# One fused Mamba-2 and FFN kernel: the same steps in a new order on all four engines

## The chip, the cores and the metric

The kernel runs on one core of a Trainium2 chip. The metric is the device time of one execution in microseconds (us). Before the change three runs took 968.83, 967.83 and 967.86 us; the median is 967.86 us.

## The reference, cut to what matters

The input is 4 sequences of 1024 rows with 256 numbers each. Two sublayers follow one another, each as `x + layernorm(f(layernorm(x)))`.

```python
# f of the first sublayer: a Mamba-2 block, chunks of the scan, 8 heads of 64, state 128
zxbcdt = u @ in_proj_kernel                     # 256 -> 1288: z, xBC, dt
xBC = silu(causal_conv1d(xBC, w, b))            # 4 taps
dt = softplus(dt + dt_bias); dA = dt * -exp(A_log)
Y = Y_diag(C, B, exp(segsum(dA)), x*dt) + Y_off(C, state, exp(cumsum(dA))) + x*D
y = Y * silu(z); y = y * rsqrt(mean(y*y) + EPS) * norm_weight
return y @ out_proj_kernel
# f of the second sublayer: gated FFN, 2048 hidden, weights packed in 4 bits with scales
gelu = 0.5 * gate * (1 + tanh(0.797885 * (gate + 0.044715 * gate**3)))
return (gelu * up) @ Wd.T
```

## The kernel before

**Blocks.** The 4096 rows are cut into blocks of 512, shifted by half a block, so there are 9 of them (`NBLK`); the first and the last have one half only. A block's attention part is done in two halves of 256 rows, with two chunks of 128 in each. The FFN of a block runs over 16 slices of the hidden size (`NT`). In the text "attention" stands for the Mamba sublayer.

**Steps.** Everything is written as steps with a name and a number, one function for each step and engine. An order, written out by hand as a string, says which steps an engine takes one after the other. `name:k<` belongs to the block before, `name:k` to this one, `name:k>` to the next and `>>` to the one after. `drive` runs the orders `FIRST`, then `ORDER` for i = 2 to 8, then `LAST`. `there` leaves out the steps of halves that don't exist. Each engine (TensorE "pe", ScalarE "act", VectorE "dve", GpSimd "pool") runs its own order; they meet only in semaphores. The DMA queue of SyncE has its own fixed list.

**Steps of the attention half j.** `stats1`, `xn`, `xt`, `xn_split` normalise and transpose the input. `ip:0` to `ip:2` (half 0) and `ip:3` to `ip:5` (half 1) are the input projection, `taps` and `conv` the convolution, `silu` its activation. `z` and `gate` are the gate's projection; `z:3` and `z:4` also give dt, which `dt_bias` and `softplus` finish. `cs`, `decays`, `ct`, `sums`, `exps`, `decay_sums` and `decay_matrix` make the decays; a DMA spreads the sums over the partitions. `gb`, `gb_copy`, `decayed_products`, `xtr`, `xdt`, `yo`, `yoff`, `yd`, `ydiag`, `st` and `state` are the scan; `yt`, `yt_split`, `square`, `out`, `stats2`, `ln2` the output projection, norm and residual; `x1n`, `x1t`, `x1_split` normalise and transpose for the FFN.

**Steps of the FFN slice n.** TensorE's `gu:n` makes gate and up. ScalarE's `gelu:n` reads the gate, VectorE's `inter:n` multiplies by up, ScalarE's `split:n` and GpSimd's `split:n` make the high and low parts, TensorE's `dn:n` multiplies with the down weights. `fin` and `ln4` close the block. Matmuls run in three passes over high and low parts. In the first stage `dq`, `scale` and `dl` unpack the 12 pieces of the FFN weights; `wi_split`, `wi_z`, `wo_split` and `wo_lo` split the other weights, `rates` prepares A.

**Banks.** PSUM has three banks for the attention (`mb`), three for gate and up (`fb`), two for the FFN's output (`db`). The n-th use of a kind in TensorE's `ORDER` takes bank n % 3 and waits for the reader of the use three before:

```python
m_bank = {use[:2]: mb[n % 3] for n, use in enumerate(m_uses)}
f_bank = {use[:2]: fb[n % 3] for n, use in enumerate(f_uses)}
```

So `up:n` waits for `gelu:n-1`, and gate n for `inter:n-2`. A few waits more that the text speaks of:

```python
def gelu(f, par, n):
    act.wait_ge(s["gate"], count("gate", f, n))
    wait_before(act, "lo", f, n - 2)          # GpSimd's split of two slices before
def ip(i, par, q):                            # TensorE
    if isinstance(i, int) and i == 0 and q == 3:
        pe.wait_ge(wi_ready, 2)               # VectorE's wi_split
```

Of the kernel before, what the change touches and what calls it, by code (L numbers as in the profile page):

```python
# [78 lines left out]
        decay_matrix:0 decay_matrix:1 decay_matrix:2 split:3< split:4< gb_copy:0 decay_matrix:3 gelu:5< split:5<  # L79
        yt_split:0 square:0 gelu:6< gelu:7< yt_split:1 split:6< xn_split:1 split:7< taps:3 square:1 gelu:8<  # L80
        gate:3 gate:4 dt_bias:1 gelu:9< split:8< taps:4 taps:5 gelu:10< split:9< gate:5 gelu:11< silu:3 silu:4
        silu:5 decay_matrix:4 decay_matrix:5 split:10< gb_copy:1 exps:1 decay_matrix:6 gelu:12< split:11<
        xn_split:0> decay_matrix:7 square:2 gelu:13< yt_split:2 split:12< gelu:14< split:13< gelu:15< split:14<
        square:3 yt_split:3 split:15< dt_bias:0> gate:0> x1_split:0 gate:1> x1_split:1 taps:0> taps:1> taps:2>""",
    "dve": """
        inter:0< decays:0 inter:1< conv:1 inter:2< conv:2 sums:0 xdt:0 decay_sums:0 inter:3< decay_sums:1
        inter:4< gb_copy:0 decay_sums:2 decay_sums:3 decayed_products:0 stats1:1 yoff:0 ydiag:0 inter:5<
        decayed_products:1 state:0 yt_split:0 xdt:1 stats2:0 xn:1 yoff:1 ln2:0 ydiag:1 inter:6< inter:7< state:1
        yt_split:1 xn_split:1 stats2:1 dt_bias:1 ln2:1 conv:3 softplus:1 inter:8< stats1:0> decays:1 inter:9<
        conv:4 inter:10< xn:0> conv:5 sums:1 inter:11< decay_sums:4 decay_sums:5 decay_sums:6 gb_copy:1  # L90
        decayed_products:2 xdt:2 yoff:2 inter:12< x1n:0 xn_split:0> decay_sums:7 ydiag:2 decayed_products:3
        x1n:1 state:2 yt_split:2 xdt:3 inter:13< stats2:2 yoff:3 inter:14< ln2:2 ydiag:3 state:3 yt_split:3
        inter:15< stats2:3 x1n:2 dt_bias:0> ln2:3 softplus:0> x1n:3 fin:0< x1_split:0 x1_split:1 conv:0> ln4:0<""",
    "pool": """
# [18 lines left out]
        taps:5 dq:5 silu:3 dl:1 dl:2 silu:4 dq:6 gate:5 dq:7 dq:8 silu:5 wo_split:0 dl:3 dl:4 exps:1
        decay_sums:4 decay_sums:5 gb_copy:1 decay_matrix:4 decay_matrix:5 decay_sums:6 dq:9 dq:10 xn_split:0>
        decay_matrix:6 decay_sums:7 dl:5 square:2 yt_split:2 decay_matrix:7 square:3 yt_split:3 dl:6 dt_bias:0>
        gate:0> gate:1> taps:0> taps:1> silu:0> x1_split:1 dl:7 dq:11 taps:2> silu:1> gate:2> gelu:0 gelu:1
        silu:2> exps:0> split:0 decay_sums:0> decay_sums:1> decay_matrix:0> decay_matrix:1> gb_copy:0>
        decay_sums:2> split:1 decay_matrix:2> gelu:2 decay_sums:3> split:2 gelu:3 dl:8 square:0> split:3
        yt_split:0> gelu:4 decay_matrix:3> gelu:5 split:4 yt_split:1> gelu:6 split:5 xn_split:1> gelu:7
# [1163 lines left out]
```

## Time and profile before

| | before |
|---|---|
| median of the runs | 967.86 us |
| profiled execution, its own time | 965.19 us |
| its span, first to last instruction | 963.1 us |
| TensorE busy | 880.5 us (91%) |
| VectorE busy | 751.7 us (78%) |
| ScalarE busy | 614.1 us (64%) |
| GpSimd busy | 355.0 us (37%) |

In the rows PE is TensorE, DVE VectorE, ACT ScalarE, POOL GpSimd, SP SyncE. A row of a timeline has the start, the time taken, the engine, the source line, the operation, what it writes and reads, the count of merged instructions, and in brackets the idle time of the engine before it with what ended that. Merged instructions overlap, so the cost of a step is read from its start to the next one's start. The first stage ends, and the first round of `ORDER` begins, at 179.2 us; a full round takes 109.4 us; `LAST` begins at 919.7 us.

### The profile page before, as it was taken

To read this page: it belongs to the slowest core of one execution; us is meant where nothing else is said; L and a number is where in the kernel's file an instruction comes from. 1 tells how busy PE (TensorE), PEld (TensorE's weight loads), DVE (VectorE), ACT (ScalarE), POOL (GpSimd) and SP (SyncE) were. 2 spreads that over 40 slices of the span, in tenths; PEclk is the share of its full clock that TensorE was granted. 3 is DMA by queue.
4 is the path that set the end of the run, shared out by engine and by line. 5 is a ranking of instruction groups with operands and counts; after the bars stand their busy time and mean duration, and the time that the engine had idled before them with its cause. 6 is when DMAs were issued, how large, how long until landed. Compare 5 with 4: busy or idle time off the path is not lost.

```text
span 963.1 us, 17495 instructions
## 1 busy us (share of the span) xinstructions
PE 880.5 (91%) x6304; PEld 767.2 (80%) x6304; DVE 751.7 (78%) x2031; ACT 614.1 (64%) x1031; POOL 355.0 (37%) x342
## 2 busy tenths in 40 slices
...
DMA packets 19205, 34.57 MB, mean 36 GB/s; under 512 B 2480, under 2 KB 11440, under 8 KB 19120
## 3 DMA queue, kind: packets, MB, share of 16 engines
...
q10 hardware_dynamic: 864, 0.03, 0.1%
HBM read 29.14 MB, written 4.33 MB: 35 GB/s over the span
## 4 chain that ended last, share of the span: by engine, by line
PE 63%; DVE 15%; ACT 13%; issue 5%; POOL 3%; DMA 1%; SPq 0%; POOLq 0%; ACTq 0%; DVEq 0%
PE fb L1082 28%; PE db L1082 14%; PE mb L1082 10%; DVE xc L890 3%; PE mb L1191 3%; ACT L710 3%; PE mb L1182 2%; POOL hl L588 2%; ACT hid L710 2%; PE mb L1172 2%; ACT xc L670 2%; PE mb L1197 1%; ACT xc L663 1%; DVE st L1007 1%; ACT lmat L652 1%
## 5 line engine op out<-in xcount | busy, mean ns | idle before, releaser
L588 POOL TENSOR_TENSOR hl<-hid,hl 128x512 fp32r<-128x512 f32 (+1 forms) x144 | 182.7, 1273 | 336.1 <-ACT hl L717 336.1
L1082 PE MATMUL fb<-x1t,wg 128*128 128x512 f32 (+1 forms) x864 | 215.9, 386 | 3.2 <-DVE x1t L993 2.7
L1082 PE MATMUL fb<-x1t,wu 128*128 128x512 f32 (+1 forms) x864 | 203.2, 371 | 16.3 <-ACT hid L710 16.3
L1082 PE MATMUL db<-wd,hl 128*128 128x256 f32 x1536 | 217.5, 291 | 0.7 <-POOL hl L588 0.7
L1082 PEld LDWEIGHTS db<-wd,hl 128*128 128x128 f32 x1536 | 196.2, 191 | 14.7 <-issue 9.8
L1082 PEld LDWEIGHTS fb<-x1t,wu 128*128 128x128 f32 x864 | 150.6, 190 | 51.5 <-ACT hid L710 25.4
L1082 PEld LDWEIGHTS fb<-x1t,wg 128*128 128x128 f32 x864 | 147.6, 191 | 36.4 <-issue 11.6
L710 ACT ACTIVATE hid<-fb 128x512 f32<-128x512 f32 (+1 forms) x144 | 78.5, 550 | 135.1 <-PE fb L1082 119.5
L890 DVE SCALAR_TENSOR_TENSOR xc<-raw,cw,xc 128x256 f32<-128x256 f32 x288 | 135.7, 539 | 6.8 <-ACT xc L663 4.8
L999 DVE TENSOR_TENSOR hid<-fb,hid 128x512 f32<-128x512 f32 (+1 forms) x144 | 90.1, 626 | 60.7 <-PE fb L1082 34.4
L558 POOL TENSOR_TENSOR rs<-ve,neg_half 128x1 f32<-128x1 f32 (+2 forms) x89 | 61.9, 696 | 175.6 <-DVE ve L792 68.5
L717 ACT ACTIVATE hl<-hid 128x512 fp32r<-128x512 f32 (+1 forms) x144 | 82.1, 580 | 56.9 <-DVE hid L999 40.1
L710 ACT ACT_TABLE_LOAD x65 | 83.4, 1283 | 25.3 <-POOL hl L588 24.5
L1082 PE MATMUL mb<-xnt,wi 128*128 128x256 f32 x576 | 79.5, 289 | 13.8 <-ACT sz L678 9.0
L1082 PEld LDWEIGHTS mb<-xnt,wi 128*128 128x128 f32 x576 | 74.3, 195 | 15.3 <-issue 14.7
L567 POOL TENSOR_TENSOR xdd<-xdt,ex 128x512 f32<-128x512 f32 x32 | 34.4, 1076 | 82.4 <-ACT ex L634 64.9
L1082 PE MATMUL mb<-wi,xnt 128*128 128x264 f32 (+1 forms) x384 | 52.3, 285 | 0.2 <-ACT xc L663 0.2
L1082 PE MATMUL mb<-wo,yt 128*128 128x256 f32 x384 | 51.6, 283 | 0.0
L864 DVE TENSOR_SCALAR lmat<-lmat,ct_ 128x128 f32<-128x128 f32 x208 | 51.6, 316 | 0.0
L1082 PEld LDWEIGHTS mb<-wo,yt 128*128 128x128 f32 x384 | 47.9, 189 | 1.8 <-issue 1.0
L663 ACT ACTIVATE xc<-mb,cb,cw 128x256 f32<-128x256 f32 x96 | 49.2, 573 | 0.0
L1082 PEld LDWEIGHTS mb<-wi,xnt 128*128 128x128 f32 x384 | 48.3, 189 | 0.4 <-issue 0.4
...
## 6 DMA issues: line engine op xcount, KB each, us to landing
...
xin<-in_u SPq DMA_DIRECT2D x16, 256.0 KB, 2.7
out<-xb SPq DMA_DIRECT2D x16, 256.0 KB, 2.3
wg_raw<-in_packed SPq DMA_DIRECT2D x4, 256.0 KB, 12.4
wg_raw<-in_scales SPq DMA_DIRECT2D x4, 256.0 KB
wu_raw<-in_packed SPq DMA_DIRECT2D x4, 256.0 KB, 12.1
wu_raw<-in_scales SPq DMA_DIRECT2D x4, 256.0 KB
wd_raw<-in_packed SPq DMA_DIRECT2D x4, 256.0 KB, 11.9
```

Of the source, the lines that this page charges most:

```text
L558: pool.tensor_tensor(dst, src, neg_half[:, 0:src.shape[1]], ALU.pow).then_inc(s["rstd" + name], 1)
L567: pool.tensor_tensor(per_head(xdd[:]), per_head(xdt[:]), spread_heads(ex[:, q // 2, 1, q % 2, :]), ALU.mult).then_inc(s["xdd"], 1)
L588: pool.tensor_tensor(hl[:, hs, n % 2, 1, :], hid[:, hs, n % 2, :], hl[:, hs, n % 2, 0, :].bitcast(F32), ALU.subtract).then_inc(s["lo"], 1)
L663: last = act.activation(xc[:, ct, :], ps[:, e, :], ACT.Identity, bias=cb[:, ct:ct + 1], scale=cw[:, ct, TAPS - 1:TAPS])
L670: act.activation(xc[:, 2 * pr:2 * pr + 2, :], xc[:, 2 * pr:2 * pr + 2, :], ACT.Silu).then_inc(s["xc"], 1)
L710: act.activation(hid[:, halves(f), n % 2, :], by_half(f_bank["gate", n], f), ACT.Gelu_apprx_tanh).then_inc(s["gelu"], 1)
L717: act.activation(hl[:, halves(f), n % 2, 0, :], hid[:, halves(f), n % 2, :], ACT.Copy).then_inc(s["hi"], 1)
L864: last = dve.tensor_scalar(lmat[:, c, h0 + h, :], lmat[:, c, h0 + h, :], ct_[:, 0, r:r + 1], 0.0, ALU.subtract, ALU.min)
L890: ins = dve.scalar_tensor_tensor(out=xc[:, ct, :], in0=raw[:, slot, e, tap:tap + SUB], scalar=cw[:, ct, tap:tap + 1], in1=xc[:, ct, :], op ...
L999: dve.tensor_tensor(hid[:, halves(f), n % 2, :], by_half(f_bank["up", n], f), hid[:, halves(f), n % 2, :], ALU.mult).then_inc(s["inter"], 1)
L1082: last = pe.matmul(ps, lhs(a, k), rhs(b, k), start=start and n == 0, stop=stop and n == len(todo) - 1, skip_group_check=check)
L1191: pe.matmul(m_bank["st", q][:], gb[:, 2 + c, :], xdd[:], start=True, stop=True).then_inc(s["st"], 1)
```

## The change

The four strings in `ORDER` and in `FIRST` and the strings of TensorE and ScalarE in `LAST` hold the same steps in another order. No step is added or taken away, and no function changes. Banks are dealt out by position in TensorE's `ORDER`; the attention uses and the FFN uses keep their order among themselves in `ORDER`. The diff, cut to the places that the text speaks of (each string is one line of steps; "..." marks what is left out):

```diff
 ORDER = {
     "pe": """
-        gu:0< gu:1< cs:0 gu:2< ct:0 dn:0< gu:3< xtr:0 gu:4< dn:1< gb:0 dn:2< gu:5< yo:0 yd:0 dn:3< st:0 gu:6<
-        yt:0 xtr:1 dn:4< out:0 yo:1 dn:5< yd:1 st:1 gu:7< xt:1 yt:1 gu:8< ip:3 out:1 z:3 z:4 dn:6< gu:9< dn:7<
-        ip:4 cs:1 ip:5 gu:10< ct:1 z:5 gu:11< gu:12< dn:8< gb:1 yo:2 dn:9< xtr:2 xt:0> gu:13< dn:10< yd:2 dn:11<
-        st:2 yt:2 xtr:3 gu:14< out:2 yo:3 dn:12< yd:3 st:3 gu:15< yt:3 dn:13< x1t:0 out:3 z:0> z:1> dn:14<
-        dn:15< ip:0> x1t:1 ip:1> z:2> ip:2>""",
+        cs:0 gu:0< gu:1< gu:2< dn:0< gu:3< ct:0 xtr:0 gb:0 gu:4< dn:1< yo:0 dn:2< yd:0 dn:3< st:0 gu:5< yt:0
+        xtr:1 gu:6< out:0 dn:4< yo:1 yd:1 dn:5< st:1 xt:1 gu:7< yt:1 ip:3 gu:8< out:1 z:3 dn:6< z:4 gu:9< ip:4
+        cs:1 ip:5 dn:7< z:5 ct:1 gu:10< gu:11< gb:1 dn:8< yo:2 xtr:2 dn:9< xt:0> gu:12< dn:10< yd:2 st:2 gu:13<
+        yt:2 xtr:3 dn:11< out:2 yo:3 yd:3 dn:12< gu:14< st:3 yt:3 gu:15< out:3 dn:13< x1t:0 z:0> z:1> dn:14<
+        dn:15< x1t:1 ip:0> ip:1> z:2> ip:2>""",
     "act": """
-        gelu:0< gelu:1< split:0< silu:0 gelu:2< silu:1 gate:2 split:1< split:2< gelu:3< silu:2 gelu:4< exps:0
+        gelu:0< gelu:1< split:0< silu:0 gelu:2< silu:1 split:1< gate:2 silu:2 split:2< gelu:3< gelu:4<
+        decay_matrix:0 exps:0 decay_matrix:1 split:3< gb_copy:0 decay_matrix:2 gelu:5< split:4< yt_split:0
...
+        decay_matrix:7 gelu:12< split:11< split:12< yt_split:2 gelu:13< square:2 square:3 gelu:14< split:13<
+        yt_split:3 gelu:15< split:14< split:15< dt_bias:0> x1_split:0 gate:0> x1_split:1 gate:1> taps:0> taps:1>
+        taps:2>""",
     "dve": """
...
+        yt_split:0 decay_sums:3 xdt:1 decayed_products:1 stats2:0 yoff:1 ln2:0 ydiag:1 xn_split:1 state:1
...
+        x1n:1 xdt:2 decayed_products:2 xn_split:0> yoff:2 decay_sums:7 inter:11< ydiag:2 state:2 inter:12<
+        decayed_products:3 yt_split:2 inter:13< xdt:3 yoff:3 stats2:2 ydiag:3 ln2:2 inter:14< yt_split:3
+        stats2:3 state:3 inter:15< ln2:3 dt_bias:0> x1n:2 x1n:3 softplus:0> fin:0< x1_split:0 x1_split:1 conv:0>
+        ln4:0<""",
     "pool": """
+        split:0< split:1< split:2< stats1:1 xdt:0 split:3< yoff:0 split:4< xdt:1 stats2:0 split:5< yoff:1
+        split:6< split:7< ln2:0 stats2:1 split:8< ln2:1 stats1:0> split:9< xdt:2 split:10< yoff:2 split:11<
+        xdt:3 split:12< yoff:3 stats2:2 ln2:2 split:13< split:14< stats2:3 split:15< ln2:3 fin:0<""",
 FIRST = {
     "pe": """
-        xt:1 ip:3 ip:4 z:3 z:4 z:5 ip:5 cs:1 xtr:2 ct:1 gb:1 yo:2 st:2 xt:0> yd:2 xtr:3 yt:2 yo:3 yd:3 out:2
+        xt:1 ip:3 ip:4 z:3 z:4 cs:1 ip:5 ct:1 z:5 gb:1 xtr:2 yo:2 xt:0> st:2 yd:2 yt:2 xtr:3 yo:3 out:2 yd:3
...
     "act": """
-        wi_split:0 wi_z:0 xn_split:1 rates:0 taps:3 taps:4 dq:0 dq:1 dl:0 dq:2 dt_bias:1 gate:3 gate:4 dq:3 dq:4
+        wi_split:0 wi_z:0 xn_split:1 rates:0 dq:0 dq:1 taps:3 taps:4 gate:3 gate:4 dt_bias:1 dq:2 dq:3 dq:4
...
     "dve": """
-        stats1:1 xn:1 wi_split:0 xn_split:1 rates:0 conv:3 wo_split:0 dt_bias:1 dq:0 scale:0 dq:1 scale:1 dq:2
-        scale:2 dl:0 stats1:0> dq:3 scale:3 conv:4 dq:4 dq:5 softplus:1 xn:0> dq:6 dq:7 scale:4 decays:1 conv:5
-        dq:8 scale:5 dl:2 wo_lo:0 dl:3 xdt:2 sums:1 dl:1 gb_copy:1 yoff:2 decayed_products:2 scale:6 state:2
-        ydiag:2 xn_split:0> xdt:3 yt_split:2 decayed_products:3 scale:7 yoff:3 ydiag:3 stats2:2 yt_split:3 ln2:2
-        state:3 dq:9 stats2:3 x1n:2 dt_bias:0> ln2:3 softplus:0> x1n:3 conv:0> decays:0> scale:8 x1_split:1
+        stats1:1 xn:1 xn_split:1 wi_split:0 rates:0 dt_bias:1 dq:0 stats1:0> wo_split:0 softplus:1 decays:1
+        scale:0 dq:1 dq:2 scale:1 dq:3 xn:0> conv:3 scale:2 conv:4 wo_lo:0 conv:5 dq:4 dl:1 dl:0 scale:3 sums:1
+        gb_copy:1 xdt:2 yoff:2 decayed_products:2 state:2 xn_split:0> dq:5 ydiag:2 decayed_products:3 scale:4
+        yt_split:2 scale:5 xdt:3 yoff:3 stats2:2 ydiag:3 ln2:2 state:3 yt_split:3 dq:6 x1n:2 stats2:3 dt_bias:0>
+        ln2:3 softplus:0> x1n:3 conv:0> x1_split:1 decays:0> conv:1> conv:2> dl:2 sums:0> scale:6 xdt:0> inter:0
...
-        stats2:3> inter:14 dt_bias:0>> ln2:3> x1n:2> inter:15 x1n:3> softplus:0>> x1_split:0> conv:0>>
-        x1_split:1> fin:0 ln4:0""",
+        inter:14 ln2:3> softplus:0>> inter:15 x1_split:0> x1n:2> x1n:3> conv:0>> x1_split:1> fin:0 ln4:0""",
 LAST = {
     "pe": """
-        dn:7< gu:10< gu:11< dn:8< dn:9< gu:12< gu:13< dn:10< dn:11< gu:14< dn:12< gu:15< dn:13< dn:14< dn:15<""",
+        gu:9< gu:10< dn:8< dn:9< gu:11< gu:12< gu:13< dn:10< dn:11< gu:14< gu:15< dn:12< dn:13< dn:14< dn:15<""",
```

## Rows read from the trace of the kernel before

**Rows 1.** Windows: length; busy time of PE, PEld, DVE, ACT, POOL; clock; DMA share, GB/s.
```profile
0.00:87.06 87.06, 38.92 (x256) 31.59 (x256) 69.42 (x170) 55.67 (x102) 16.31 (x25) 0.78 0.37 116
87.06:179.10 92.04, 81.06 (x667) 72.94 (x666) 83.10 (x216) 72.46 (x149) 34.75 (x38) 0.94 0.10 30
...
507.15:616.50 109.35, 107.33 (x767) 93.06 (x766) 90.39 (x250) 72.57 (x115) 43.22 (x39) 1.00 0.09 30
...
919.67:963.10 43.43, 36.59 (x288) 35.98 (x288) 12.48 (x36) 11.74 (x32) 12.91 (x18) 0.93 0.05 19
```

**Rows 2.** Timeline of TensorE in one full round.
```profile
511.84 1.65 PE L1082 MATMUL fb<-x1t,wu 128*128 128x512 f32 x6 [0.41 <-ACT hid L710]
...
523.37 1.65 PE L1082 MATMUL fb<-x1t,wu 128*128 128x512 f32 x6 [0.64 <-ACT hid L710]
...
570.38 1.55 PE L1082 MATMUL fb<-x1t,wg 128*128 128x512 f32 x6
...
573.12 1.52 PE L1082 MATMUL fb<-x1t,wg 128*128 128x512 f32 x6
...
583.42 1.66 PE L1082 MATMUL fb<-x1t,wu 128*128 128x512 f32 x6 [0.79 <-ACT hid L710]
```

**Rows 3.** Timeline of ScalarE at the start of that round.
```profile
508.37 0.60 ACT L660 ACTIVATE raw<-mb 128x512 f32<-128x512 f32 x1 [1.88 <-DVE hist L901]
...
509.89 1.28 ACT L710 ACT_TABLE_LOAD   x1
511.19 1.09 ACT L710 ACTIVATE hid<-fb 128x512 f32<-128x512 f32 x2
```

**Rows 4.** Timeline of VectorE in the first 30 us.
```profile
7.68 1.76 DVE L757 TENSOR_TENSOR wi<-wi_raw,wi 128x1536 fp32r<-128x1536 f32 x1 [0.88 <-ACT wi L602]
...
10.21 0.69 DVE L806 TENSOR_TENSOR xnt<-mb,xnt 128x512 fp32r<-128x512 f32 x1 [0.68 <-ACT xnt L621]
12.49 0.17 DVE L765 TENSOR_SCALAR a_neg<-a_neg 128x8 f32<-128x8 f32 x1 [1.59 <-ACT a_neg L613]
...
15.60 2.46 DVE L890 SCALAR_TENSOR_TENSOR xc<-raw,cw,xc 128x256 f32<-128x256 f32 x6 [2.73 <-ACT xc L663]
...
19.60 0.42 DVE L1034 TENSOR_SCALAR wg_raw<-wg_raw 128x512 int32<-128x512 int32 x1
...
20.78 1.29 DVE L1046 TENSOR_TENSOR wg_raw<-wg_raw 128x512 f32<-128x512 f16 x2
...
26.77 1.22 DVE L1052 TENSOR_TENSOR wg<-wg_raw,wg 128x1024 fp32r<-128x1024 f32 x1
```

**Rows 5.** Timeline of TensorE in the first 32 us.
```profile
11.04 4.70 PE L1082 MATMUL mb<-xnt,wi 128*128 128x256 f32 x24 [3.01 <-DVE xnt L806]
```

**Rows 6.** Timeline of SyncE's queue: when the second piece's words are asked for.
```profile
4.36 0.47 SPq L508 DMA_DIRECT2D wu_raw<-in_packed  x1
```

**Rows 7.** DMA issues of the page: count, KB each, median us from issue to landing.
```profile
wu_raw<-in_packed SPq DMA_DIRECT2D x4, 256.0 KB, 12.1
```

**Rows 8.** Timeline of VectorE before the first `gu`: this row is `x1_split:1`.
```profile
86.38 0.68 DVE L993 TENSOR_TENSOR x1t<-fb,x1t 128x512 fp32r<-128x512 f32 x1
```

**Rows 9.** Groups by line: count, busy us and mean ns of one, then idle before.
```profile
L588 POOL TENSOR_TENSOR hl<-hid,hl 128x512 fp32r<-128x512 f32 (+1 forms) x144 | 182.7, 1273 | 336.1 <-ACT hl L717 336.1
...
L576 POOL TENSOR_TENSOR yg<-yg,t 128x512 f32<-128x512 f32 x32 | 43.3, 1354 | 0.0
```

**Rows 10.** Timeline of TensorE at the end of the last stage.
```profile
954.47 0.98 PE L1082 MATMUL db<-wd,hl 128*128 128x256 f32 x6 [0.16 <-POOL hl L588]
955.69 0.97 PE L1082 MATMUL db<-wd,hl 128*128 128x256 f32 x6 [0.24 <-POOL hl L588]
```

**Rows 11.** Timeline of VectorE in a full round: this row is one `conv`.
```profile
566.76 4.33 DVE L890 SCALAR_TENSOR_TENSOR xc<-raw,cw,xc 128x256 f32<-128x256 f32 x6
```

**Rows 12.** Timeline of GpSimd in the same stretch.
```profile
566.49 1.31 POOL L588 TENSOR_TENSOR hl<-hid,hl 128x512 fp32r<-128x512 f32 x1
569.13 1.29 POOL L588 TENSOR_TENSOR hl<-hid,hl 128x512 fp32r<-128x512 f32 x1 [1.33 <-ACT hl L717]
```

More of the change, by code:

```diff
@@ L77 @@
-    "act": """
-        gelu:0< gelu:1< split:0< silu:0 gelu:2< silu:1 gate:2 split:1< split:2< gelu:3< silu:2 gelu:4< exps:0
[L79 to L84, printed above, removed]
@@ L85 @@
-    "dve": """
[L86 to L93, printed above, removed]
+        cs:0 gu:0< gu:1< gu:2< dn:0< gu:3< ct:0 xtr:0 gb:0 gu:4< dn:1< yo:0 dn:2< yd:0 dn:3< st:0 gu:5< yt:0
@@ new lines @@
+    "dve": """
+        decays:0 inter:0< conv:1 inter:1< conv:2 inter:2< stats1:1 sums:0 decay_sums:0 xdt:0 decay_sums:1
+        gb_copy:0 inter:3< decayed_products:0 yoff:0 decay_sums:2 ydiag:0 inter:4< state:0 xn:1 inter:5<
+        yt_split:0 decay_sums:3 xdt:1 decayed_products:1 stats2:0 yoff:1 ln2:0 ydiag:1 xn_split:1 state:1
+        inter:6< inter:7< yt_split:1 conv:3 stats2:1 inter:8< ln2:1 dt_bias:1 softplus:1 stats1:0> x1n:0
+        decays:1 conv:4 inter:9< conv:5 sums:1 decay_sums:4 decay_sums:5 inter:10< xn:0> decay_sums:6 gb_copy:1
+        x1n:1 xdt:2 decayed_products:2 xn_split:0> yoff:2 decay_sums:7 inter:11< ydiag:2 state:2 inter:12<
+        decayed_products:3 yt_split:2 inter:13< xdt:3 yoff:3 stats2:2 ydiag:3 ln2:2 inter:14< yt_split:3
+        stats2:3 state:3 inter:15< ln2:3 dt_bias:0> x1n:2 x1n:3 softplus:0> fin:0< x1_split:0 x1_split:1 conv:0>
+        ln4:0<""",
```

71 lines of the change are left out of this document (35 added, 36 removed).

## The prediction

> **What bounds the kernel now.** I read the stages first (the windows), then TensorE's own waits, then the order of time on VectorE and ScalarE at the places where those waits end. The windows [rows 1] cut the run where TensorE starts the `gu` of a new block. In one full round of the repeated block TensorE is busy 107.3 of 109.35 us; VectorE is busy 90.4 and ScalarE 72.6. So six full rounds and a short one are TensorE's, and an order can win back only what TensorE waits. The first stage is different: up to 87.06 us VectorE is busy 69.4 us and TensorE 38.9, and from there to 179.10 us VectorE is busy 83.1 of 92.0. That stage belongs to VectorE and to chains that run through it. The last stage (43.4 us) is TensorE again.
>
> TensorE's waits in a full round are three, all of one kind: `up:n` may not start before `gelu:n-1` has emptied its bank. They are 0.41, 0.64 and 0.79 us, 1.84 together [rows 2]. The first shows the pattern [rows 3]: `taps:2` waits 1.88 us for `conv:0`'s history, then comes a table load of 1.28 us, then `gelu:0`.
>
> **The change, part by part.** No instruction is removed or added by name; only positions change, so every stage keeps its work. What changes by itself is the number of function table loads on ScalarE: a walk through the order (gelu, silu and exponential functions alternate) gives 21 a round before and 19 after, and 21 before and 26 after in the first stage. At 1.28 us a load [rows 3] that is 2.6 us less per round on an engine with 36 us idle, and 6.4 us more in the first stage on an engine that was busy 55.7 + 72.5 = 128.1 of 179.1 us [rows 1]: 134.5 does not make it the bound, so neither is a term. The Trainium skill (ScalarE: Activation LUTs, What ACT_TABLE_LOAD costs) prices a switch at 1.28 us plus about 1.38 us of drain; here the activation starts 0.02 us behind the load's end [rows 3], so the drain is not seen, and by its price the first stage would have 13 us more on ScalarE, still not the bound.
>
> *First stage, up to the first `gu`.* Three moves act in the first 20 us. VectorE's `wi_split` (1.76 us and a small one, 7.68 to about 9.5 [rows 4]) now stands behind `xn_split:1`, which ended at 10.90, so it ends near 12.75, and `ip:3`, which needs it and started at 11.04 [rows 5], starts 1.7 us later. ScalarE's `taps:3` now stands behind `dq:0` and `dq:1`; the words of `dq:1` land at 4.36 + 12.1 = 16.5 us [rows 6, 7], its two passes end near 17.6 and `taps:3` near 19.0. `z:4` goes into the bank that `taps:3` empties, so it ends near 20.0, and VectorE's next step is `dt_bias:1`, which needs it. VectorE thus stands still from 12.8 to 20.0, 7.2 us; before it waited 1.6 and 2.7 us there and did `conv:3` in between [rows 4]. Added idle: 2.9 us. `softplus:1` and `decays:1` come right behind with their chain through ScalarE and TensorE, 1.2 us more. Further on eight fillers no longer stand between the steps of the attention chain (`dq:7` to `9`, `scale:6` to `8`, `dl:2`, `dl:3`); where a filler is gone the step waits for its partner. I take 2.8 us for all those places (bounds 0 and 6: nothing if other fillers cover them, four waits of 1.5 if not). On the other side `x1_split:1` has those eight and `decays:0` behind it instead of ahead: 3 x 1.18 + 3 x 1.29 + 2 x 1.22 + 0.2 = 10.0 us of VectorE work [rows 4]. So it ends at 87.06 - 10.0 + 2.9 + 1.2 + 2.8 = 83.9 us [rows 1, 8], and TensorE's first `gu` starts 3 us earlier than now.
>
> *First stage, from there on.* The 10.0 us are only put off. VectorE has 83.1 + 10.0 = 93.1 us of work left and the next block's `gu:0` needs its last one, so the stage ends at 83.9 + 93.1 = 177.0 plus idle. Idle was 8.9 us; with a larger backlog fewer steps find VectorE waiting, but `conv:0>` now stands right behind `x1n:3` and waits for `split:15` and `taps:0`. I take 6 (bounds 3 and 11): 183.0 against 179.1, +3.9 us, from +0.9 to +8.9. TensorE has 81 us of work in these 99 us, so its own waits cost nothing by themselves.
>
> *Repeated block.* I followed the new order once round on all four engines with the durations of rows and counted TensorE in steps: `gu` 2.74 us from start to start [rows 2], and the others likewise. The three old waits go down, and places that had slack become tight. With T the start of `gu:0`: `gelu:0` ends near 4.3 and `up:1` is reached at 4.1, wait 0.2. `up:4` needs `gelu:3`, which now stands behind `silu:1`, `gate:2`, `silu:2` and `split:2`: wait 0.3. `dn:5` needs POOL's `split:5`, which now stands behind `stats2:0`: POOL can't do it until `out:0`'s statistics are there; wait 0.25. `cs:1` and `ip:5` need `dt_bias:1`, `softplus:1` and `gate:3`, `gate:4` behind a table load: 0.55. `dn:9` 0.1; `yd:2` needs `yoff:2`, now behind `xn_split:0>`: 0.35. `st:3` goes into the bank that `ln2:2` empties, and from `yo:3` the way is POOL's `split:12` (1.27) and two more passes (the second 1.35) [rows 9], then `ydiag:3`, then `ln2:2`: 0.3. Sum 2.05; my steps come 1.6 us short of TensorE's true round, which gives the chains that much air, about 0.25 of it at these places: 1.8 us. Against 1.84 before that is no change: 0 us over some 6.7 rounds. Bounds: all new waits vanish, -1.84 x 6.7 = -12.3; or POOL and VectorE collide at two of them (below), +1.7 x 6.7 = +11.
>
> *Last stage.* At the end `dn:14` and `dn:15` wait 0.16 and 0.24 us for POOL's `split` [rows 10]. Now `dn:12` too stands behind `gu:15` and covers 0.72 us. -0.4 us, bounds -1 and +0.5.
>
> The sum is +3.9 + 0 - 0.4 = **+3.5 us**. The profiled execution took 965.2 us (span 963.1), 2.7 below the median of the runs, 967.9; I add the sum to the median: **971.4 us**, slower. What a measurement of this kernel can tell from no change is 0.2%, 1.9 us: 965.9 to 969.8.
>
> **The rivals.**
> *The loop wins its waits back.* For it: there is 36 us of idle time on ScalarE and 19 on VectorE in a round, two loads fewer, and the places above are tight by 0.1 to 0.5 us, about the error of a count by rows. If they all close, the round is 107.5 us and the time 971.4 - 12.3 = 959.1; if half, 965. It decides as soon as a round's waits are below 1.84 - (3.5 + 1.9) / 6.7 = 1.0 us. Against it: there are seven such places and each is a separate chain. Chance 0.32.
> *Collisions of POOL and VectorE.* A pair's six passes in `conv` take 2.46 us alone [rows 4], but 4.33 us while POOL's two `split` ran for 1.31 and 1.29 us [rows 11, 12]: 1.87 us lost. The Trainium skill (SBUF — State Buffer, Who interferes with whom) says that a VectorE instruction with two SBUF inputs and a GpSimd instruction that reads SBUF block one another for a whole instruction; the trace agrees in kind, 1.87 lost for 2.60 shared. In the new order `split:0` falls into `conv:1`, `split:11` beside `decayed_products:3`, and `yoff:2` beside `decay_sums:7`; the last two stand directly before `dn:11` and `gu:13`. At 0.5 to 1.3 us each and one to two of them on the path, a round grows by 1.0 us: 978. Against: the new order frees two `conv` from POOL. Chance 0.18.
> *The first stage does not lose.* If the fillers that remain cover all places and the later idle falls to 3 us, it ends at 177 us and the time is 967 to 968, the same as now. For it: VectorE is the bound there and its work is unchanged. Against: the 7.2 us standstill rests on a landing and a bank, both fixed. Chance 0.20, and with it the case that losses and gains cancel.
> My forecast keeps 0.30.
>
> **How the numbers follow.** Slower is the forecast and the collisions, 0.30 + 0.18 = 0.48; faster the first rival, 0.32; same the third, 0.20. The range reaches from the middle of the loop's gain, 960, to a loop with collisions and the first stage's upper half, 981. The forecast's own range is 969 to 975.
>
> **What would show it.** Right: on VectorE a gap of some 7 us between `rates` and `dt_bias:1`; `x1_split:1` near 84 us; TensorE's second-block `gu:0` at 182 to 184 us (179.2 before); a round of 109 to 109.7 us with waits at `up:1`, `up:4`, `dn:5`, `cs:1` and `st:3` instead of three; 19 loads a round. Wrong: a round below 108.5 us, or a first stage at or below 179 us; a round above 110.5 would point to the collisions.

## The result

Seven runs of the changed kernel took 968.39 to 972.70 us, median 970.84; seven of the kernel before 965.20 to 968.83, median 966.99. The ratio is 1.0038, with an interval of 1.0022 to 1.0054: slower by 0.4%, about 4 us. The interval is clear of 1, and the difference is 3.9 us between the medians. The profiled execution took 970.27 us, its span 968.5. A ratio below is always to the kernel before, run again beside the kernels of its group.

### The profile page after: what moved, and what is told of

Read it like the earlier page. It is cut to its first block, busy times and chain, and to the rows that moved or that the text cites. A ratio compares the mean times of both kernels' runs of the same rounds, so it can differ in the third digit from the quotient of the medians.

```text
span 968.5 us, 17486 instructions
## 1 busy us (share of the span) xinstructions
PE 886.3 (92%) x6304; PEld 768.0 (79%) x6304; DVE 768.4 (79%) x2031; ACT 606.7 (63%) x1022; POOL 350.9 (36%) x342
## 4 chain that ended last, share of the span: by engine, by line
PE 65%; DVE 17%; ACT 9%; issue 5%; DMA 2%; POOL 1%; SPq 0%; DVEq 0%; POOLq 0%; ACTq 0%
PE fb L1082 27%; PE db L1082 14%; PE mb L1082 14%; DVE lmat L864 3%; DVE xc L890 3%; ACT L710 3%; PE mb L1172 2%; PE mb L1182 2%; PE mb L1191 2%; ACT hid L710 1%; PE mb L1197 1%; PE mb L1163 1%; DMA lmat<-rows 1%; ACT L652 1%; ACT xc L663 1%
## 5 line engine op out<-in xcount | busy, mean ns | idle before, releaser
L1082 PE MATMUL db<-wd,hl 128*128 128x256 f32 x1536 | 213.9, 289 | 3.4 <-POOL hl L588 2.8
L1082 PE MATMUL fb<-x1t,wg 128*128 128x512 f32 (+1 forms) x864 | 211.8, 381 | 4.3 <-DVE x1t L993 2.7
L890 DVE SCALAR_TENSOR_TENSOR xc<-raw,cw,xc 128x256 f32<-128x256 f32 x288 | 125.6, 505 | 9.2 <-ACT xc L663 8.0
L558 POOL TENSOR_TENSOR rs<-ve,neg_half 128x1 f32<-128x1 f32 (+2 forms) x89 | 57.2, 643 | 148.6 <-DVE ve L962 54.2
L864 DVE TENSOR_SCALAR lmat<-lmat,ct_ 128x128 f32<-128x128 f32 x208 | 74.4, 422 | 0.5
L652 ACT ACTIVATE lmat<-lmat 128x512 f32<-128x512 f32 x64 | 39.8, 627 | 50.0 <-DVE lmat L864 49.6
L909 DVE TENSOR_TENSOR lmat<-lmat,gb 128x1024 f32<-128x1024 f32 x32 | 52.6, 1643 | 3.4 <-ACT lmat L652 3.2
L1082 PEld LDWEIGHTS mb<-wo,yt 128*128 128x128 f32 x384 | 50.6, 195 | 3.3 <-issue 1.0
```

The lines of the kernel that those rows point to most:

```text
L558: pool.tensor_tensor(dst, src, neg_half[:, 0:src.shape[1]], ALU.pow).then_inc(s["rstd" + name], 1)
L652: act.activation(part, part, ACT.Exp, scale=sign).then_inc(s["lmat"], 1)
L864: last = dve.tensor_scalar(lmat[:, c, h0 + h, :], lmat[:, c, h0 + h, :], ct_[:, 0, r:r + 1], 0.0, ALU.subtract, ALU.min)
L890: ins = dve.scalar_tensor_tensor(out=xc[:, ct, :], in0=raw[:, slot, e, tap:tap + SUB], scalar=cw[:, ct, tap:tap + 1], in1=xc[:, ct, :], op ...
L909: dve.tensor_tensor(lmat[:, c, :, :], lmat[:, c, :, :], gb[:, c, :].unsqueeze(1).broadcast_to([P, HEADS, CH]), ALU.mult).then_inc(s["m"], 1)
L1082: last = pe.matmul(ps, lhs(a, k), rhs(b, k), start=start and n == 0, stop=stop and n == len(todo) - 1, skip_group_check=check)
```

## The profile after

The windows of the changed kernel, cut at the same places as [rows 1]: the end of block 0's `x1_split:1`, the end of the first stage, one full round, and the last stage. The stage ends where TensorE starts the first step of `ORDER`, which was `gu:0<` and in the new order is `cs:0` (the `gu:0<` behind it starts at 185.66). The columns are as there.

```profile
0.00:83.81 83.81, 37.34 (x244) 31.35 (x244) 60.12 (x155) 51.44 (x94) 15.46 (x25) 0.82 0.38 120
83.81:185.30 101.49, 86.10 (x680) 77.26 (x679) 93.08 (x230) 82.30 (x160) 36.24 (x38) 0.92 0.08 27
185.30:294.78 109.48, 108.08 (x766) 92.74 (x765) 91.74 (x251) 68.98 (x112) 43.18 (x40) 1.00 0.08 28
...
925.30:968.50 43.20, 35.35 (x288) 34.75 (x288) 12.50 (x37) 12.14 (x32) 13.00 (x18) 0.96 0.06 19
```

`x1_split:1` ends 3.3 us earlier than before and the stage ends 6.2 us later. VectorE is busy 60.1 + 93.1 = 153.2 us of it, 152.5 before; so its idle time grew from 26.6 to 32.1 us. The full round is as long as it was, with another kind of waiting in it (below).

VectorE in the first 30 us of the changed kernel, the place of [rows 4]:

```profile
9.58 0.69 DVE L806 TENSOR_TENSOR xnt<-mb,xnt 128x512 fp32r<-128x512 f32 x1 [2.86 <-ACT xnt L621]
10.19 2.97 DVE L757 TENSOR_TENSOR wi<-wi_raw,wi 128x1536 fp32r<-128x1536 f32 x1
...
19.92 0.17 DVE L813 TENSOR_TENSOR spa<-mb,dtb 128x8 f32<-128x8 f32 x1 [6.59 <-PE mb L1082]
20.55 0.17 DVE L813 TENSOR_TENSOR spa<-mb,dtb 128x8 f32<-128x8 f32 x1 [0.47 <-PE mb L1082]
...
24.56 0.17 DVE L823 TENSOR_SCALAR spw<-spe 128x16 f32<-128x16 f32 x1 [0.37 <-ACT spl L629]
...
26.97 0.29 DVE L843 COPY csr<-mb 128x128 f32<-128x128 f32 x1 [0.91 <-PE mb L1123]
```

The row at 19.92 is `dt_bias:1`: VectorE stands from 13.3 to 19.9 us, then 0.47, 0.37 and 0.91 us more. The row at 10.19 is `wi_split`, and it takes 2.97 us where it took 1.76 [rows 4]. GpSimd does its own part of `wi_split` in the same time, and TensorE's `ip:3` waits for VectorE's. GpSimd's timeline of the changed kernel, then TensorE's, where [rows 5] is the row of before:

```profile
9.14 2.40 POOL L552 TENSOR_TENSOR wi<-wi_raw,wi 128x1024 fp32r<-128x1024 f32 x1 [3.19 <-ACT wi L607]
```

```profile
13.30 5.49 PE L1082 MATMUL mb<-xnt,wi 128*128 128x256 f32 x24 [5.34 <-DVE wi L760]
18.59 1.93 PE L1082 MATMUL mb<-wi,xnt 128*128 128x264 f32 x12
```

In the repeated block the three waits of [rows 2] are gone. The longest wait of TensorE is now at `yd:2`, and the second at `up:13`. First TensorE, then VectorE in the same round of the changed kernel:

```profile
367.78 1.60 PE L1082 MATMUL db<-wd,hl 128*128 128x256 f32 x12
370.13 1.15 PE L1182 MATMUL mb<-xdt,lmat 128*64 128x64 f32 x32 [0.75 <-DVE t L926]
371.21 1.13 PE L1191 MATMUL mb<-xdd,gb 128*128 128x512 f32 x2
372.46 1.66 PE L1082 MATMUL fb<-x1t,wg 128*128 128x512 f32 x6
374.43 1.65 PE L1082 MATMUL fb<-x1t,wu 128*128 128x512 f32 x6 [0.31 <-ACT hid L710]
```

```profile
364.69 1.75 DVE L909 TENSOR_TENSOR lmat<-lmat,gb 128x1024 f32<-128x1024 f32 x1
368.70 0.69 DVE L806 TENSOR_TENSOR xnt<-mb,xnt 128x512 fp32r<-128x512 f32 x1 [2.25 <-ACT xnt L621]
369.30 0.68 DVE L926 TENSOR_TENSOR t<-mb,ex 128x512 f32<-128x512 f32 x1
```

The last row is `yoff:2`. It stands behind `xn_split:0>` (368.70), for which VectorE waits 2.25 us; `yd:2` goes into the bank that `yoff:2` reads. The rounds, measured from one round's first step on TensorE to the next, are 109.5, 109.3, 110.9, 109.2, 109.2, 109.5 and a short one of 82.6 us; before they were 109.1, 109.6, 109.2, 109.3, 109.5, 109.4 and 84.3. Together they changed by -0.4 us.

One round of six is 1.4 us longer, in every kernel here that has the new `ORDER` untouched. In it, TensorE waits 0.96 us at `cs:1`. VectorE's `ln2:1` in the round before and in that round, then GpSimd's `split` of slice 8 in the same two rounds:

```profile
344.55 0.35 DVE L975 TENSOR_SCALAR xb<-xb,mr 128x256 f32<-128x256 f32 x1
...
454.52 1.41 DVE L975 TENSOR_SCALAR xb<-xb,mr 128x256 f32<-128x256 f32 x1
```

```profile
344.98 1.29 POOL L588 TENSOR_TENSOR hl<-hid,hl 128x512 fp32r<-128x512 f32 x1 [1.18 <-ACT hl L717]
...
454.50 1.29 POOL L588 TENSOR_TENSOR hl<-hid,hl 128x512 fp32r<-128x512 f32 x1 [0.72 <-ACT hl L717]
```

The two passes of L975 differ by such a meeting with GpSimd. Three groups of the page after have other mean times than before, with the same work: `conv` (L890) got cheaper, from 539 to 505 ns, and `decay_sums` (L864) and `decayed_products` (L909) dearer, from 316 and 1228 ns. That these too are meetings with GpSimd fits their rows (the two passes of L909 that lie clear of GpSimd take 1.22 us each, the longest beside it 2.33), but no experiment separated them.

```profile
L890 DVE SCALAR_TENSOR_TENSOR xc<-raw,cw,xc 128x256 f32<-128x256 f32 x288 | 125.6, 505 | 9.2 <-ACT xc L663 8.0
...
L864 DVE TENSOR_SCALAR lmat<-lmat,ct_ 128x128 f32<-128x128 f32 x208 | 74.4, 422 | 0.5
...
L909 DVE TENSOR_TENSOR lmat<-lmat,gb 128x1024 f32<-128x1024 f32 x32 | 52.6, 1643 | 3.4 <-ACT lmat L652 3.2
```

## The experiments: which part of the change costs

Four kernels differ only in which of the three dictionaries is new. The kernel before took 966.42 us beside them. In kernels that I wrote the line numbers are one higher than in the rows above. In the diffs from here on a line shows one stretch of a string of steps and may be cut at both ends.

**Old `FIRST`, new `ORDER` and `LAST`.** Against the changed kernel:

```diff
 FIRST = {
     "pe": """
-        xt:1 ip:3 ip:4 z:3 z:4 cs:1 ip:5 ct:1 z:5 gb:1 xtr:2 yo:2 xt:0> st:2 yd:2 yt:2 xtr:3 yo:3 out:2 yd:3
+        xt:1 ip:3 ip:4 z:3 z:4 z:5 ip:5 cs:1 xtr:2 ct:1 gb:1 yo:2 st:2 xt:0> yd:2 xtr:3 yt:2 yo:3 yd:3 out:2
...
```

> The changed kernel with the first stage's order of before; ORDER and LAST stay new. My theory (the loss is made in the first stage, the loop is even): the first stage ends at 179 to 180 us again, full rounds stay at 109.3 us, and the time is 5 to 7 us below the changed kernel's, that is 964 to 966, some 1 to 2 us below the kernel before. Rival (the loss is the loop's, through collisions): the time stays at 969 to 972.

Measured: 966.70 us, ratio 0.9998 to the kernel before (0.9990 to 1.0007), so even with it and not 1 to 2 us below, as I had expected. The stage ends at 180.5 us.

**New `FIRST` alone.** The edit against the kernel before is the other way round:

```diff
 FIRST = {
     "pe": """
-        xt:1 ip:3 ip:4 z:3 z:4 z:5 ip:5 cs:1 xtr:2 ct:1 gb:1 yo:2 st:2 xt:0> yd:2 xtr:3 yt:2 yo:3 yd:3 out:2
+        xt:1 ip:3 ip:4 z:3 z:4 cs:1 ip:5 ct:1 z:5 gb:1 xtr:2 yo:2 xt:0> st:2 yd:2 yt:2 xtr:3 yo:3 out:2 yd:3
...
```

> The kernel before with the new FIRST alone. My theory: the second block's first gu at 185 us instead of 179, the rest unchanged, 972 to 974 us. Rival (the two orders hide each other's ends, and the late start is made up in the loop): under 970.

Measured: 970.68 us, ratio 1.0041 (1.0025 to 1.0056). The stage ends at 183.5 us. I had expected 185 and 972 to 974 us. This part alone costs what the whole change costs. The windows of the first stage, of the kernel with the old `FIRST` and then of this one:

```profile
0.00:88.47 88.47, 41.67 (x256) 33.73 (x256) 69.94 (x170) 55.77 (x102) 16.34 (x25) 0.75 0.36 114
88.47:180.47 91.99, 81.23 (x668) 73.32 (x667) 83.01 (x215) 72.36 (x148) 34.76 (x38) 0.94 0.10 30
```

```profile
0.00:83.54 83.54, 38.12 (x246) 32.01 (x247) 60.63 (x157) 51.91 (x94) 15.41 (x25) 0.82 0.38 120
83.54:183.54 100.00, 83.02 (x678) 74.29 (x678) 93.12 (x229) 82.30 (x161) 36.29 (x38) 0.95 0.09 28
```

**New `ORDER` alone.** Against the kernel before:

```diff
 ORDER = {
     "pe": """
-        gu:0< gu:1< cs:0 gu:2< ct:0 dn:0< gu:3< xtr:0 gu:4< dn:1< gb:0 dn:2< gu:5< yo:0 yd:0 dn:3< st:0 gu:6<
+        cs:0 gu:0< gu:1< gu:2< dn:0< gu:3< ct:0 xtr:0 gb:0 gu:4< dn:1< yo:0 dn:2< yd:0 dn:3< st:0 gu:5< yt:0
...
```

> The kernel before with the new ORDER alone. My theory: full rounds even at 109.3 us, the short eighth round 1.7 us shorter: 965 to 967 us. Rival (the loop loses to the collisions of VectorE and GpSimd at yd:2 and gu:13): 970 or more.

Measured: 966.06 us, ratio 0.9992 (0.9983 to 1.0002). The stage ends at 181.6 us.

**New `LAST` alone.** Against the kernel before:

```diff
 LAST = {
     "pe": """
-        gu:0< gu:1< gu:2< gu:3< dn:0< dn:1< gu:4< dn:2< gu:5< dn:3< gu:6< dn:4< gu:7< gu:8< dn:5< dn:6< gu:9<
+        gu:0< gu:1< gu:2< dn:0< gu:3< dn:1< gu:4< dn:2< gu:5< dn:3< gu:6< dn:4< gu:7< dn:5< dn:6< gu:8< dn:7<
...
```

> The kernel before with the new LAST alone. My theory: dn:12 behind gu:15 covers part of the last wait, -0.3 us in the last stage (43.1 for 43.4): no difference that the runs can tell. Rival (two gu on end make a new wait for inter): +0.5 us or more in the last stage.

Measured: 966.39 us, ratio 1.0005 (0.9993 to 1.0016); the last stage takes 43.2 us instead of 43.4. What follows from the four: the loss is in `FIRST`, and `ORDER` and `LAST` are each even. The seven profiles with the old `FIRST` end the stage between 179.2 and 181.7 us (mean 180.5), the changed kernel and the one with the new `FIRST` alone at 185.3 and 183.5; so the 6.2 us between the first pair of profiles holds some 2 us of chance in the start, and 4 us of change. Where most of that chance comes from is seen in the next section.

## The experiments: what in the first stage costs

All four start from the changed kernel. The kernel before took 967.38 us beside them.

**`wi_split` back ahead of `xn_split:1`.**

```diff
 FIRST, "dve":
-        stats1:1 xn:1 xn_split:1 wi_split:0 rates:0 dt_bias:1
+        stats1:1 xn:1 wi_split:0 xn_split:1 rates:0 dt_bias:1
```

> The changed kernel with one move of the first 13 us undone: VectorE does wi_split before xn_split:1 again. What the prediction said: z:4 waits for taps:3, which stays behind dq:0 and dq:1, so z:4 ends near 19.5 as now and nothing is won. Rival, from the trace of the changed kernel (taps:3 ended at 18.3, before TensorE had come to z:4 at 19.6): wi_split is what sets it, ip:3 starts near 10.4 instead of 13.3, z:4 near 18.3, the gap before dt_bias:1 ends 1.2 us earlier, and the time falls by some 1 us.

Measured: 969.51 us, ratio 1.0028 (1.0015 to 1.0041). Its interval overlaps with that of the changed kernel (1.0022 to 1.0054), so the runs don't show a gain. `wi_split` is two passes on VectorE. The first is back at its old length, the second, small one is not, and `dt_bias:1` comes at 18.69:

```profile
7.88 1.76 DVE L758 TENSOR_TENSOR wi<-wi_raw,wi 128x1536 fp32r<-128x1536 f32 x1 [1.14 <-ACT wi L603]
9.56 2.31 DVE L761 TENSOR_TENSOR wi<-wi_raw,wi 128x16 fp32r<-128x16 f32 x1
...
18.69 0.17 DVE L814 TENSOR_TENSOR spa<-mb,dtb 128x8 f32<-128x8 f32 x1 [6.14 <-PE mb L1083]
```

The small pass took 0.17 us in the kernel before. Here GpSimd's part of `wi_split` began at 8.98, ahead of it, and ran to 11.84. So `ip:3` starts at 12.62, not near 10.4 as I had expected (11.04 before, 13.30 in the changed kernel): the move traded one meeting for another, and it did so in the next two kernels with `wi_split` back as well. The old `FIRST` has this meeting at times too. In five of its seven profiles the small pass takes 0.17 us and the stage ends at 179.2 to 180.5; in the other two, the new `ORDER` alone and the kernel with both moves of the last section, it takes 2.31 and 2.32, and the stage ends at 181.6 and 181.7, the two latest. The means of the two sets are 1.7 us apart, and that is most of the chance in the start. GpSimd's part waits for ScalarE's, which began at 7.32 and 7.72 us in these two and at 8.30 to 8.91 in the five, each time behind a wait for the DMA of its piece except at 7.32.

**`taps:3` and `taps:4` back ahead of `dq:0` and `dq:1`.**

```diff
 FIRST, "act":
-        wi_split:0 wi_z:0 xn_split:1 rates:0 dq:0 dq:1 taps:3 taps:4 gate:3
+        wi_split:0 wi_z:0 xn_split:1 rates:0 taps:3 taps:4 dq:0 dq:1 gate:3
```

> The changed kernel with the other move undone: ScalarE does taps:3 and taps:4 before dq:0 and dq:1. By the prediction z:4 then starts 1.5 us earlier and the time falls by that. Rival: TensorE is not at z:4 before 19.6 us because ip:3 started late, so the gap before dt_bias:1 ends where it does now and the time stays.

Measured: 971.87 us, ratio 1.0053 (1.0033 to 1.0073), no better than the changed kernel. VectorE of this kernel, `wi_split`, `dt_bias:1`, `dq:0` and `softplus:1`:

```profile
10.83 2.92 DVE L758 TENSOR_TENSOR wi<-wi_raw,wi 128x1536 fp32r<-128x1536 f32 x1
...
19.59 0.17 DVE L814 TENSOR_TENSOR spa<-mb,dtb 128x8 f32<-128x8 f32 x1 [5.68 <-PE mb L1083]
...
21.32 0.43 DVE L1035 TENSOR_SCALAR wg_raw<-wg_raw 128x512 int32<-128x512 int32 x1 [0.73 <-ACT wg_raw L725]
...
26.11 0.17 DVE L824 TENSOR_SCALAR spw<-spe 128x16 f32<-128x16 f32 x1 [1.42 <-ACT spl L630]
```

`dt_bias:1` hardly moves (19.92 to 19.59), though `ip:3` started at 13.88 here and 13.30 there. That `taps:3` did not hold `z:4` is seen in the changed kernel itself: there `taps:3` ended at 18.28, before TensorE came to `z:3` at 18.59. And `dq:0` and `dq:1` now stand between `taps` and ScalarE's `dt_bias:1`: `softplus:1` is 1.5 us later than in the changed kernel.

**Both back.**

```diff
 FIRST, "act":
-        rates:0 dq:0 dq:1 taps:3 taps:4 gate:3
+        rates:0 taps:3 taps:4 dq:0 dq:1 gate:3
 FIRST, "dve":
-        xn:1 xn_split:1 wi_split:0 rates:0
+        xn:1 wi_split:0 xn_split:1 rates:0
```

> Both moves undone. If each holds z:4 up to a point of its own (18.3 and 19.6), only both together bring it back to 16.3 to 17.2 us: the gap before dt_bias:1 shrinks from 6.6 to about 4 us of waiting, x1_split:1 ends 2 to 3 us earlier, and the time falls by 2 to 3 us. Rival: the gain up to x1_split:1 is lost to other waits later in the first stage, and the second block's first gu stays within 1 us of where it is.

Measured: 970.55 us, ratio 1.0033 (1.0021 to 1.0046): the 2 to 3 us that I had expected are not there. `dt_bias:1` is at 18.2 us and the gap before it 5.0, with the small pass at 2.31 us and `ip:3` at 12.37. The stage ends at 187.6 us in the profile, the latest of all, but that execution took 972.79 us, 2.2 above the median.

**Both back, and `conv:3` into the gap.** As the last one, and on VectorE:

```diff
 FIRST, "dve":
-        rates:0 dt_bias:1 dq:0
...
-        xn:0> conv:3 scale:2 conv:4
+        rates:0 conv:3 dt_bias:1 dq:0
...
+        xn:0> scale:2 conv:4
```

> Both moves undone and conv:3 put back behind rates on VectorE, where it fills the gap. Theory (VectorE's work sets the first stage's end, so 2.8 us of work moved into a gap is 2.8 us won, less 1 us by which dt_bias:1 is later): 1.5 to 3 us below the kernel with both moves undone, about the time of the kernel before or lower. Rival (the chain of the attention half sets x1_split:1, not VectorE's work): no more than 0.5 us below it.

Measured: 969.24 us, ratio 1.0019 (1.0006 to 1.0032). VectorE does `conv:3` at 16.80, ahead of `dt_bias:1` as in the kernel before (15.60), and has 12.2 us of idle time up to `softplus:1`, against 15.3 in the changed kernel and 11.4 before. By the medians that is 1.3 us below the kernel with both moves undone, a little under the 1.5 to 3 expected, and about half of the loss. The intervals of this kernel and of the changed one overlap, so the half is an estimate. The profiled execution has the small pass at 2.31 us again.

**Steps put into the gaps of the changed kernel.** The kernel before took 967.61 us beside it.

```diff
 FIRST, "dve":
-        rates:0 dt_bias:1 dq:0 stats1:0> wo_split:0 softplus:1
+        rates:0 wo_split:0 stats1:0> dt_bias:1 dq:0 softplus:1
...
-        sums:1 gb_copy:1 xdt:2
+        sums:1 dq:5 gb_copy:1 xdt:2
...
-        yoff:3 stats2:2
+        yoff:3 dq:6 stats2:2
```

> The kernel after the change, with four steps of VectorE in FIRST put into its gaps: wo_split:0 and stats1:0> ahead of dt_bias:1 (a gap of 6.6 us), dq:5 ahead of gb_copy:1 (1.6 us), dq:6 ahead of stats2:2 (1.8 us). Theory (the first stage ends with VectorE's 153 us of work plus its idle time): 2.4 + 1.15 + 1.15 = 4.7 us less idle up to x1_split:1, so x1_split:1 ends near 79.5 to 80.5 us instead of 83.8, and TensorE's second-block gu:0 starts about 4 us earlier than in the kernel after the change; the time is 966.5 to 968, the same as before the change. Rival (the chain of the steps and not VectorE's total sets the end, fillers are free): moving fillers shifts idle time elsewhere, the first stage ends within 1 us of 183.5 and the time is 970 to 971.

Measured: 971.15 us, ratio 1.0039 (1.0025 to 1.0052): nothing won, and my theory's 966.5 to 968 is wrong. VectorE and then GpSimd:

```profile
13.29 1.14 DVE L776 TENSOR_SCALAR wo_raw<-wo_raw,nw 128x256 f32<-128x256 f32 x4
19.22 0.75 DVE L788 BATCH_NORM_STATS2 st<-xin 128x6 f32<-128x256 f32 x2 [4.79 <-DMA xin<-in_u]
...
24.44 0.17 DVE L824 TENSOR_SCALAR spw<-spe 128x16 f32<-128x16 f32 x1 [2.57 <-ACT spl L630]
...
64.70 1.42 DVE L1037 SCALAR_TENSOR_TENSOR wg_raw<-wg_raw 128x512 int32<-128x512 int32 x1
```

```profile
64.28 1.28 POOL L574 TENSOR_TENSOR state<-state,ex 128x512 f32<-128x512 f32 x1
```

The rows of the next block are there only at 19.22, so `stats1:0>` fills nothing; and where the two fillers had stood, VectorE now waits 2.57 us for ScalarE, whose `dt_bias:1` ends at the same time as ever. Idle time up to `softplus:1` is 15.2 us, as it was (15.3). The two `dq` do fill their gaps (idle time up to `x1_split:1` 21.9 instead of 23.7 us), but `dq:6` meets GpSimd's `state` there and takes 1.42 us for a pass of 0.69. The profile shows the stage 0.8 us shorter, the runs show no difference.

## The experiments: the repeated block

These have the old `FIRST` with the new `ORDER` and `LAST`, which was even with the kernel before, and one or two moves on VectorE. The kernel before took 967.61 us beside them.

**`yoff:2` ahead of `xn_split:0>`.**

```diff
 ORDER, "dve":
-        x1n:1 xdt:2 decayed_products:2 xn_split:0> yoff:2 decay_sums:7 inter:11<
+        x1n:1 xdt:2 decayed_products:2 yoff:2 xn_split:0> decay_sums:7 inter:11<
```

> The old FIRST with the new ORDER and LAST (measured 0.9998 of the kernel before), and in VectorE's ORDER yoff:2 ahead of xn_split:0>. Theory (yd:2 waits 0.75 us in each round only because yoff:2 stands behind xn_split:0>): the wait at yd:2 goes, a round is 0.6 to 0.7 us shorter, and the time is 962.5 to 964, ratio 0.996 to 0.998. Rival (the wait moves: xn_split:0> 0.7 us later makes TensorE wait at another step, or yoff:2 meets a split of GpSimd): the round stays within 0.2 us of 109.2 and the time at 966 to 967.

Measured: **958.06 us, ratio 0.9908 (0.9895 to 0.9922)**, the fastest of all kernels here. TensorE, then VectorE, then the window of one full round:

```profile
361.35 1.59 PE L1083 MATMUL db<-wd,hl 128*128 128x256 f32 x12
362.86 1.15 PE L1183 MATMUL mb<-xdt,lmat 128*64 128x64 f32 x32
363.94 1.13 PE L1192 MATMUL mb<-xdd,gb 128*128 128x512 f32 x2
364.74 1.71 PE L1083 MATMUL fb<-x1t,wg 128*128 128x512 f32 x6
366.71 1.65 PE L1083 MATMUL fb<-x1t,wu 128*128 128x512 f32 x6 [0.26 <-ACT hid L711]
```

```profile
359.93 0.68 DVE L927 TENSOR_TENSOR t<-mb,ex 128x512 f32<-128x512 f32 x1
362.25 0.69 DVE L807 TENSOR_TENSOR xnt<-mb,xnt 128x512 fp32r<-128x512 f32 x1 [1.64 <-ACT xnt L622]
```

```profile
288.54:396.46 107.93, 107.55 (x767) 92.66 (x766) 91.38 (x250) 70.47 (x113) 42.26 (x39) 1.00 0.09 30
```

From `dn:10` to `yd:2` TensorE takes 1.51 us (2.35 in the changed kernel), and from `st:2` to `gu:13` 0.80 us (1.25). The bank of `gu:13` waits for `inter:11`, which on VectorE stands behind `yoff:2` and `decay_sums:7`; TensorE's weight load for `gu:13` waits 0.50 us for it here and 0.95 in the changed kernel. The two savings are 0.84 + 0.45 = 1.29 us a round, and the rounds measure 107.9 to 108.2 with the one long at 109.3. I had expected 0.6 to 0.7: the wait that is marked, 0.75, was not all of what the step cost.

**`dt_bias:1` ahead of `ln2:1`.**

```diff
 ORDER, "dve":
-        stats2:1 inter:8< ln2:1 dt_bias:1 softplus:1
+        stats2:1 inter:8< dt_bias:1 ln2:1 softplus:1
```

> The old FIRST with the new ORDER and LAST, and in VectorE's ORDER dt_bias:1 ahead of ln2:1. Theory (the one round of six that is 1.4 us longer is so because ln2:1 meets GpSimd's split:8< and dt_bias:1 stands behind it): no round is over 109.6 us, the wait of 0.96 us at cs:1 is gone, and the time is 1.0 to 1.5 us less, 965.2 to 965.7 or ratio 0.9985. Rival (that round is longer for another reason): one round stays near 110.7 us and the time at 966.7.

Measured: 970.41 us, ratio 1.0038 (1.0023 to 1.0053), a miss of the expectation. The long round is gone, but now all six are long, 110.0 to 110.6 us, with 0.54 us at `cs:1` in five and 0.61 in one. So that the meeting of `ln2:1` with the `split` made the long round rests on the rows above, which agree in all eight kernels with the new `ORDER` untouched (1.41 to 1.43 us for that pass, 0.90 to 1.00 us at `cs:1`), and not on this experiment. VectorE, then GpSimd:

```profile
340.14 0.17 DVE L814 TENSOR_TENSOR spa<-mb,dtb 128x8 f32<-128x8 f32 x1 [1.09 <-PE mb L1083]
340.34 1.16 DVE L818 SCALAR_TENSOR_TENSOR spn<-spa 128x16 f32<-128x16 f32 x1
...
343.26 0.16 DVE L824 TENSOR_SCALAR spw<-spe 128x16 f32<-128x16 f32 x1
```

```profile
340.17 1.29 POOL L589 TENSOR_TENSOR hl<-hid,hl 128x512 fp32r<-128x512 f32 x1 [1.18 <-ACT hl L718]
```

`dt_bias:1` has to wait 1.09 us for TensorE's `z:4`, which `ln2:1` had covered; its pass of L818 (0.17 us alone, 0.36 in the kernel without the move, where it meets the end of the `split`) meets nearly all of the `split` and takes 1.16; and `softplus:1` (343.26) then stands behind `ln2:1`, where it started at 341.84 without the move. A step put ahead of another so that it should not be held up by it held itself up.

**Both moves.**

```diff
 ORDER, "dve":
-        stats2:1 inter:8< ln2:1 dt_bias:1 softplus:1
+        stats2:1 inter:8< dt_bias:1 ln2:1 softplus:1
...
-        decayed_products:2 xn_split:0> yoff:2 decay_sums:7
+        decayed_products:2 yoff:2 xn_split:0> decay_sums:7
```

> Both edits of VectorE's ORDER together, with the old FIRST. If they add up: -0.65 x 6 - 1.2 = -5 us, time near 961.5 to 962.5, ratio 0.995. If the first is given back elsewhere in the round: 965 to 966.

Measured: 962.97 us, ratio 0.9956 (0.9941 to 0.9971). The sum comes out near the expectation, but for another reason. Against the ratio of 0.9998 without moves, the one move is worth -0.0090 and the other +0.0040; together they give 0.9948, near the 0.9956 measured. The rounds are 108.7 to 109.4 us. Each move is worth about the same with and without the other.

## Why the prediction came out as it did

The forecast was +3.5 us, and the measured ratio is 1.0038, +3.7. The place is right: the first stage loses and the loop is even. That the total fits so closely is in part luck, since two errors offset each other: the forecast put the stage's end at 183.0 us and the two kernels measured 185.3 and 183.5, and the profile of before, from which the 3.9 us were counted, ends the stage earliest of seven (179.2, mean 180.5). By its own steps:

- **The start gap**: `dt_bias:1` at 19.9 us (20.0 forecast) and `softplus:1` and `decays:1` have 0.37 and 0.91 us of new waiting (1.2 forecast). The instant is right, and one of its two reasons is wrong. I had `z:4` held by the bank of `taps:3`, at 19.0, but `taps:3` ended at 18.28; the kernel with `taps` put back has `dt_bias:1` 0.3 us earlier only, and the one with `wi_split` put back 1.2 us. `z:4` waits its turn on TensorE behind `ip:3`, which started 2.3 us later and not 1.7, because `wi_split` met GpSimd's part and took 2.97 us. That is the mechanism of my collision rival, in a place where I had not looked for it.
- **`x1_split:1`**: 83.8 us, forecast 83.9. The steps put off are as counted: VectorE was busy 9.3 us less, 10.0 counted. Added idle time 23.7 - 17.6 = 6.1 us, 6.9 summed.
- **The work from there on**: forecast 93.1 us, measured 93.1. Its idle time is the term that was mis-sized: 8.4 us, where I took 6 (bounds 3 and 11), against 8.9 before; with the new `FIRST` alone it is 6.9 (100.00 - 93.12). The backlog did not cover the waits for TensorE (1.6 and 1.3 us the longest) and for the DMA that spreads the sums (1.0), since an order is fixed and a step in front holds back all that is behind it. Two rows of the changed kernel, `sums:0` and `stats2:0`, show the two longest:

```profile
92.01 0.17 DVE L850 COPY ct_<-mb 128x16 f32<-128x16 f32 x1 [1.32 <-PE mb L1127]
...
115.58 0.43 DVE L957 BATCH_NORM_STATS2 st<-mb 128x6 f32<-128x256 f32 x1 [1.63 <-PE mb L1082]
```

So the first pair of profiles had +6.2 us where I forecast +3.9; the new `FIRST` alone gave a ratio of 1.0041, 4.0 us.

- **The repeated block**: the sum 0 is right, the list of places is not. Of seven places one showed in every round: `yd:2`, forecast 0.35 and measured 0.75. `dn:9`, forecast 0.1, has a gap of 0.15 at most. `up:1`, `up:4`, `dn:5` and `st:3` did not wait, and `cs:1` only in one round, for a collision. `up:13` with its 0.31 I did not list. I had named `yd:2`'s reason, `yoff:2` behind `xn_split:0>`, and the experiment shows it to be worth 1.3 us a round and 0.9% in all (0.9998 to 0.9908, 8.7 us). That is most of the 12.3 us that the rival of a faster loop needed. The 958 us were measured with the old `FIRST`; with the new one, some 4 us dearer, it would be about 962 by estimate, so the 959 of that rival was not reached even then. The short round's -1.7 us was not forecast; it offsets the one long round's +1.4.
- **Table loads**: 19 a round as forecast; in the first stage 27 where 26 were forecast and 23 (not 21) before. They decide nothing.
- **The last stage**: -0.2 us for -0.4. `dn:14` waits 0.65 us for GpSimd in place of 0.16 and 0.24 [rows 10]; TensorE reached the end of its work earlier and waited there.

```profile
960.43 1.71 PE L1082 MATMUL db<-wd,hl 128*128 128x256 f32 x12 [0.65 <-POOL hl L588]
```

What stays open: of the first stage's 4 us, the start gap (with the work moved back into it) is about half, by medians whose intervals overlap. How much of what is left is the meeting of `wi_split`'s small pass with GpSimd, which all three kernels with `wi_split` put back had in their profiles and five of seven with the old `FIRST` did not, is not known: no kernel kept the two apart. The rest is idle time spread over the attention chain (1.6 us at `gb_copy:1`, 1.8 at `stats2:2`) and about 1 us of longer passes on VectorE; no experiment separated these, and the one that filled two of the gaps won nothing that the runs could show.
